# Attention in forty equal slots per row: jobs placed by a table, scores first in a slot

## The chip, the cores and the metric

The kernel runs on one core of a Trainium2 chip. The metric is the device time of one execution in microseconds. The engines are TensorE (PE in the views; PEld is its weight load), VectorE (DVE), ScalarE (ACT), GpSimd (POOL) and SyncE (SP, which only starts transfers). Each engine works through its own instructions in order and waits on semaphores for the others.

## The reference

```python
x = x + 0.5 * ffn(layernorm(x))       # x: 8 rows of 1024 tokens, 256 features
x = x + attn(layernorm(x))
x = x + 0.5 * ffn(layernorm(x))

# ffn: 8 experts of width 128, exact GELU, the two best experts of each token weighted by softmax
# attn, for each row of 1024 tokens, 8 heads of 64:
#   light: q, k, v = split(layernorm(x) * g + b) @ wqkv); windows of 64 queries see the window
#          before, their own and the next; softmax; @ wo_l
#   heavy: scores x @ rt_q and x @ rt_kv; the 256 best tokens by each (argsort);
#          rms-normed rows give hq, hk, hv; full 256 x 256 attention; @ wo_h,
#          added at the places of the chosen queries
```

## The kernel before, in words

Three stages follow each other: a feed-forward stage over 16 groups of 512 tokens (`ffn_group`), the attention over 8 rows (ROWS) of 1024 tokens, and the second feed-forward stage. Each engine's program is written out by hand, and the order in which they meet is the order of these programs.

A group of the feed-forward stage has ten steps s. In s = 0 to 7 PE multiplies one expert's first layer, ACT forms the GELU twice (`hf`, `hh`), POOL their difference (`hl`, L1302), and two steps later PE multiplies the second layer and DVE adds it to `xb` (L1056). In between stand the next group's statistics, norm, transposes, routing and gate. SP stores `xb` at a group's end and loads another.

The attention works on items: one item is a pair of heads (`hp`) of one tile of 128 queries. A row has 32 items of 8 light tiles (`t < T`) and 8 of 2 heavy tiles, 40 in all. An item goes through

- `scores` (PE, L631 light and L633 heavy): two matmuls, one for each head, into three banks (NS = 3) in turn;
- `maxima` (DVE, L1168/L1170), `exps` (ACT, L883), `reciprocals` (DVE, L1186), `prob_norm` (POOL, L1335: `prob` times `rden`);
- `turn` (PE, L642: four transposes of `prob`) three slots after the scores, `turned` (the copy into `probT`, ACT for even items, DVE for odd ones);
- `values` (PE, L656) four slots after; after the fourth pair of heads `oT_s` (ACT, L899), and the out projection `op` (PE, L667) six slots after, which DVE (L1200, light) or ACT (heavy) takes away.

Beside the items there are jobs, which share banks 6 and 7 in turn (`claim` waits until the job before the last has been taken away): `zt` (transposes of `z_row` into `xt`), `qkv` 0 to 24 (projections of q, k, V, six matmuls each: L464 to L466), `srow` (router scores along a row), `ga` and `hp` (the chosen rows and their projections) and `op`. Other engines have work for a row without PE: statistics of `x1` and `y_row` (DVE, `attn_stats1/2`), `rstd` and `row_norm` (POOL), `attn_y`, `attn_z`, `attn_yr` (ACT), `dot` (DVE, L1111: the router scores of a tile), `rank_piece` (DVE, L1134 to L1140: each token's place by counting larger scores; 16 pairs of pieces per row), `places`, then `scatter` (POOL, L1322: sixteen indirect transfers of `yr` to `hs_d`), SP's load of `hrow` (L421) and `tokens`. `heavy_add` (POOL, L1331) adds the heavy output to x2 in DRAM.

A row has 44 slots (`slots`, `items_of`, `attn_jobs`): LEAD = 4 slots without an item, in which 16 projections, `srow`, `ga` and `hp` are done; then 8 slots with the heavy items of the row before and the nine projections of V, all ranks of the row and the first scatter; then 32 slots (number s) with the light items, in which the next row is prepared. For row 0 statistics and norms stand between feed-forward groups 12 to 15, and the dots and `zt` behind group 15. SP's loop over the rows stores a finished row of x2 (L436), loads the next but one (`attn_load`, L459), and loads `hrow`; after the last light item it first loads back the feed-forward weights and the first three groups.

## Time and profile before

| | |
|---|---|
| Median of 3 runs | 2230.57 us (2229.94 to 2231.97) |
| Profiled execution, its own time | 2230.17 us |
| Its span in the trace | 2228.4 us |
| Mean granted clock of TensorE | 0.976 |
| PE busy | 2059.0 us, 92% |
| DVE busy | 1522.2 us, 68% |
| ACT busy | 1264.2 us, 57% |
| POOL busy | 1045.1 us, 47% |

Times in the trace count from the first instruction. The first feed-forward stage ends near 481.5 us and the second begins at 1785.3; the attention lies between. A busy share is an average over stages, so the rows below look at stretches.

Columns of the views: a window row has its bounds and length in us, then busy us (and instructions) of PE, PEld, DVE, ACT and POOL, PE's granted clock, the DMA engines' busy share and GB/s. A timeline row has start and duration in us, engine, line, operation, output<-inputs, form and count, and in brackets the idle time before it and what ended it; neighbours alike are merged. A wait row has the waiting engine and line, what it waited for, us in total, times and the longest.
### The profile page before, as it was taken

What the parts mean: (1) busy time and instruction counts of PE and PEld (TensorE: products, weight loads), DVE (VectorE), ACT (ScalarE), POOL (GpSimd) and SP (SyncE); (2) the same over time, 40 slices, a digit from 0 to 9 for tenths busy, and PEclk for the clock granted to TensorE, in tenths of its full rate; (3) what the DMA queues carried; (4) which work ended last, traced back from release to release, by engine and by line L of the source; (5) the groups of instructions that cost most, each with busy time, mean ns of one, the idle gap of its engine ahead of it and who ended that gap; (6) DMA issues with size and microseconds to landing.
All of it is one profiled execution on the core that took longest, in us unless ns stands there. A gap on an engine that the chain in (4) does not pass through costs nothing.

```text
span 2228.4 us, 40162 instructions
## 1 busy us (share of the span) xinstructions
PE 2059.0 (92%) x13232; PEld 1594.5 (72%) x13232; DVE 1522.2 (68%) x5207; ACT 1264.2 (57%) x2948; POOL 1045.1 (47%) x1150
## 2 busy tenths in 40 slices
PE   6999999869899899898998998998999699999998
PEld 5888888856576576675665665765766478888887
DVE  6888888667647657466376375476474368888887
ACT  4555555545846746646756656557556355555554
POOL 3444444443717617527427347257164244444444
PEclk9999999889999999999999999999999799999999
DMA  6111111001002011011011021020010311111110
GB/s 224 57 58 39 46 41 40 18 20 39 11 1 86 6 48 45 1 53 39 1 58 34 1 67 25 1 74 18 1 67 6 125 24 39 39 39 39 39 39 29
DMA packets 72326, 91.17 MB, mean 41 GB/s; under 512 B 6433, under 2 KB 66233, under 8 KB 71097
## 3 DMA queue, kind: packets, MB, share of 16 engines
q1 hardware_dynamic: 61368, 69.39, 9.3%
q0 software_dynamic: 8448, 18.95, 3.0%
q8 instruction: 107, 1.75, 0.3%
q14 instruction: 99, 0.80, 0.1%
q10 hardware_dynamic: 2304, 0.28, 0.1%
HBM read 40.23 MB, written 48.37 MB: 40 GB/s over the span
## 4 chain that ended last, share of the span: by engine, by line
PE 47%; POOL 18%; DVE 17%; issue 13%; ACT 5%; DMA 0%; POOLq 0%; DVEq 0%; ACTq 0%
PE bank L464 9%; PE bank L466 9%; PE bank L465 9%; POOL prob L1335 7%; POOL hs_d L1322 4%; PE bank L667 3%; PE bank L491 3%; PE bank L601 2%; PE bank L642 2%; PE bank L631 2%; PE bank L656 2%; ACT prob L883 2%; DVE xb L1056 2%; DVE st L968 2%; POOL hl L1302 2%
## 5 line engine op out<-in xcount | busy, mean ns | idle before, releaser
L1056 DVE SCALAR_TENSOR_TENSOR xb<-bank,gate,xb 128x256 f32<-128x256 f32 x1024 | 423.9, 477 | 122.8 <-PE bank L466 122.0
L1335 POOL TENSOR_TENSOR prob<-prob,rden 128x512 f32<-128x512 f32 x320 | 348.3, 1090 | 282.1 <-DVE rden L1186 278.5
L1302 POOL TENSOR_TENSOR hl<-hf,hh 128x512 fp32r<-128x512 f32 x256 | 330.5, 1299 | 232.8 <-ACT hh L758 223.9
L1168 DVE CUSTOM_DVE_ANT_0 prob<-bank,mask 128x256 f32<-128x256 f32 x512 | 197.0, 421 | 263.3 <-PE bank L631 259.3
L757 ACT ACTIVATE hf<-bank,b1s 128x512 f32<-128x512 f32 x256 | 176.5, 689 | 338.1 <-PE bank L466 330.7
L883 ACT ACTIVATE prob<-prob,nmax 128x256 f32<-128x256 f32 x512 | 255.8, 501 | 135.2 <-DVE nmax L1168 134.2
L464 PE MATMUL bank<-w_hi,hh 128*128 128x256 f32 x1024 | 295.9, 289 | 22.6 <-POOL hl L1302 20.4
L1322 POOL DMA_INDIRECT hs_d<-yr,place x128 | 130.5, 1019 | 361.0 <-DVE place L1149 339.9
L465 PE MATMUL bank<-w_hi,hl 128*128 128x256 f32 x1024 | 290.3, 284 | 0.0
L466 PE MATMUL bank<-w_lo,hh 128*128 128x256 f32 x1024 | 290.2, 283 | 0.0
L642 PE MATMUL bank<-ident,prob 128*128 128x128 f32 x1280 | 209.3, 288 | 50.2 <-POOL prob L1335 48.0
L464 PEld LDWEIGHTS bank<-w_hi,hh 128*128 128x128 f32 x1024 | 195.3, 191 | 45.5 <-POOL hl L1302 36.7
L464 PE MATMUL bank<-xt_hi,w_hi 128*128 128x512 f32 x512 | 215.6, 421 | 8.6 <-DVE w_lo L1088 8.3
L642 PEld LDWEIGHTS bank<-ident,prob 128*128 128x128 f32 x1280 | 149.0, 144 | 104.1 <-POOL prob L1335 80.7
L465 PE MATMUL bank<-xt_hi,w_lo 128*128 128x512 f32 x512 | 203.4, 397 | 0.0
L466 PE MATMUL bank<-xt_lo,w_hi 128*128 128x512 f32 x512 | 203.2, 397 | 0.0
L465 PEld LDWEIGHTS bank<-w_hi,hl 128*128 128x128 f32 x1024 | 196.1, 191 | 6.1
L466 PEld LDWEIGHTS bank<-w_lo,hh 128*128 128x128 f32 x1024 | 196.2, 192 | 0.0
L631 PE MATMUL bank<-kT,qT 64*128 64x256 f32 x1024 | 191.0, 443 | 0.8 <-ACT V L845 0.7
L656 PEld LDWEIGHTS bank<-probT,V 128*64 128x64 f32 x2048 | 111.6, 139 | 111.6 <-issue 100.2
L656 PE MATMUL bank<-probT,V 128*64 128x128 f32 x2048 | 173.4, 291 | 19.2 <-ACT oT_s L899 16.9
L758 ACT ACTIVATE hh<-bank,b1s 128x512 fp32r<-128x512 f32 x256 | 174.4, 681 | 0.0
(165 smaller groups left out, 4333.3 us busy)
## 6 DMA issues: line engine op xcount, KB each, us to landing
xb<-in_L_attn_x SPq DMA_DIRECT2D x16, 512.0 KB, 4.0
x_d<-xb SPq DMA_DIRECT2D x16, 512.0 KB, 2.9
x<-x_d SPq DMA_DIRECT2D x8, 1024.0 KB, 5.6
x_d<-x SPq DMA_DIRECT2D x8, 1024.0 KB, 4.4
xb<-x_d SPq DMA_DIRECT2D x16, 512.0 KB, 3.9
out<-xb SPq DMA_DIRECT2D x16, 512.0 KB, 2.9
hrow<-hs_d SPq DMA_DIRECT2D x16, 257.0 KB, 2.7
w_d<-w_hi SPq DMA_DIRECT2D x2, 1024.0 KB
```

Of the source, the lines that this page charges most:

```text
L464: pe.matmul(o, w[0], x[0], start=start, stop=False)
L465: pe.matmul(o, w[1], x[0], start=False, stop=False)
L466: return pe.matmul(o, w[0], x[1], start=False, stop=stop)
L631: ins = pe.matmul(bank[g % NS][:, 0:KEYS], qT[hs, hp, t * P:(t + 1) * P], kT[hs, hp, t * P:t * P + KEYS], start=True, stop=True)
L642: ins = pe.transpose(bank[3 + j % 2][:, (2 * h + kk) * P:(2 * h + kk + 1) * P], prob[j % NP][:, h, kk * P:(kk + 1) * P], ident[:, :])
L656: ins = pe.matmul(bank[5][h * DH:(h + 1) * DH, hp * P:(hp + 1) * P], V[:, t + kk, hs] if t < T else hv[:, kk, hs], probT[j % 2][:, 2 * h + ...
L883: act.activation(prob[j % NP][:, h, :], src, ACT.Exp, bias=nmax[:, j % 4, h:h + 1], scale=-1.0 if light else 1.0, accum_out=den[:, j % 4, ...
L1056: dve.scalar_tensor_tensor(out=x, in0=bank[ob][:, (t % 2) * D:(t % 2 + 1) * D], scalar=gate[:, k % 2, t, e:e + 1], in1=x, op0=ALU.mult, op ...
L1168: ins = dve.tensor_tensor_reduce(prob[j % NP][:, h, :], bank[g % NS][:, 0:KEYS], mask[:, which, :], -1.0, 3e38, ALU.add, ALU.min, nmax[:, ...
L1302: pool.tensor_tensor(hl[i % NH][:, :], hf[i % NH][:, :], hh[i % NH][:, :].bitcast(F32), ALU.subtract).then_inc(s_hl)
L1322: pool.indirect_dma_start(hs_d[r], bass.IndirectOffsetOnAxis(place[:, b, r, t:t + 1], 0), yr[:, t, :], None).then_inc(s_sct[r], 16)
L1335: pool.tensor_tensor(prob[j % NP][:, :, :], prob[j % NP][:, :, :], rden[:, j % 4, :].unsqueeze(2).broadcast_to([P, 2, KEYS]), ALU.mult).th ...
```

## The change

The 44 slots of a row become 40, every one with an item. Slots are numbered through (u), and each job has a function that names the slot in which it stands, relative to its row's first slot; the jobs of one row may lie in slots of the row before. `QKV_AT` puts the first 13 projections into slots -20 to -2 and the rest into 0 to 15. `qkv_at` orders them so that the first half of tokens of k, q and V comes first; they are written into the same `kT`, `qT` and `V` in two halves, and scores and values wait for the projection that they need (`qkv_with`) instead of for all. In a slot PE now does scores, first job, turn, second job, values, other jobs (before: first job, turn, second job, scores, third job, values, others); ACT takes exps first. Ranks go at 32 pieces over 26 slots, in row 0 at two pieces per slot in slots 0 to 10. Row 0's statistics, norms and half of its dots move into the feed-forward groups 12 to 15. The same jobs are done; before the second feed-forward stage its first statistics, norm, transposes, logits and gate stand later (`TAIL` is slot 32 of the last row).

```diff
-LEAD, B_SLOTS = 4, 32
-A_SLOTS = LEAD + 8
-HADD = 11
-SLOTS = A_SLOTS + B_SLOTS
+LIGHT, SLOTS = 32, 40
...
+        QKV_AT = (on(-20, 2, 1, 2), on(-14, 2, 1, 2), on(-8, 2, 1, 2, 1), on(0, 1, 2, 1), on(6, 1, 1, 2), on(11, 1, 2, 1))
...
+        def rank_slot(b, i):
+
+            if b == 0:
+                return i - 10 if i < 10 else (i - 10) // 2
+            return SLOTS * b - 19 + i * 26 // 32
...
             def project(b, i):
-                if i == 0:
-                    pe.wait_ge(s_xll, 4 * b + 4)
-                    if b == 0:
-                        pe.wait_ge(s_wlo, 7)
+
+                if i in (0, 12, 13):
+                    pe.wait_ge(s_xll, 4 * b + {0: 2, 12: 3, 13: 4}[i])
+                if i == 0 and b == 0:
+                    pe.wait_ge(s_wlo, 7)
...
                 if t < T:
-                    if t == 0 and hp == 0:
-                        pe.wait_ge(*left(("qkv", b, 24)))
-                        pe.wait_ge(*left(("qkv", b, 23)))
-                        if b == 0:
-                            pe.wait_ge(s_halo, 2)
+                    if hp == 0 and t in (0, 3, 4):
+                        pe.wait_ge(s_qkv, 25 * b + {0: qkv_with(0, 0), 3: qkv_with(1, 1), 4: qkv_with(0, 1)}[t])
+                    if j == 0:
+                        pe.wait_ge(s_halo, 2)
...
-            for i in range(4):
-                z_turn(0, i)
-            for b, a in slots():
-                todo = attn_jobs(b, a)
+            for u in slots():
+                todo = attn_jobs(u)
+                if is_item(u):
+                    scores(u)
                 for what in todo[0:1]:
                     job(*what)
-                if item_back(b, a, 3) is not None:
-                    turn(item_back(b, a, 3))
+                if is_item(u - 3):
+                    turn(u - 3)
                 for what in todo[1:2]:
                     job(*what)
-                if items_of(b, a) is not None:
-                    scores(b, a)
-                for what in todo[2:3]:
-                    job(*what)
-                if item_back(b, a, 4) is not None:
-                    values(item_back(b, a, 4))
-                for what in todo[3:]:
+                if is_item(u - 4):
+                    values(u - 4)
+                for what in todo[2:]:
                     job(*what)
...
+                    if k in (12, 13) and 2 <= s < 6:
+                        attn_stats1(k - 12, s - 2)
+                    if k in (14, 15) and 2 <= s < 6:
+                        attn_stats2(k - 14, s - 2)
+                    if k == 15 and 2 <= s < 10:
+                        dot(0, (s - 2) // 2, s % 2)
...
+                    if k in (12, 13) and s == 7:
+                        rstd(1, k - 12, k - 12)
+                    if k in (14, 15) and s == 7:
+                        rstd(2, k - 14, 2 * (k - 14))
+                        row_norm(k - 14)
...
-                if b == ROWS and a == LEAD + 1:
+                if u == TAIL + 7:
                     ffn_stats(GROUPS)
```

Three places show how instructions move. The first is VectorE where row 0's first items begin (`prob`, `nmax`: maxima; `junk`, `sjunk`: rank pieces; `probT`: the copy of a turn). Before:

```order
L1138 SCALAR_TENSOR_TENSOR sjunk,rank_76<-srow,scol,later 128x128
L1140 SCALAR_TENSOR_TENSOR sjunk,rank_76<-srow,scol,not_later 128x128
L1144 TENSOR_REDUCE rank<-rank_76 128x8
L1168 ISA prob_108,nmax<-bank,mask 128x256
L1168 ISA nmax 128x1
L1168 ISA prob_108,nmax<-bank,mask 128x256
L1168 ISA nmax 128x1
L1149 CAST place<-rank 128x8
L1168 ISA prob_109,nmax<-bank,mask 128x256
L1168 ISA nmax 128x1
L1168 ISA prob_109,nmax<-bank,mask 128x256
L1168 ISA nmax 128x1
```

and now:

```order
L1203 ISA prob_108,nmax<-bank,mask 128x256
L1203 ISA nmax 128x1
L1169 TENSOR_SCALAR junk,rank_76<-srow,scol 128x640
L1171 TENSOR_SCALAR junk,rank_76<-srow,scol 128x256
L1173 SCALAR_TENSOR_TENSOR sjunk,rank_76<-srow,scol,later 128x128
L1175 SCALAR_TENSOR_TENSOR sjunk,rank_76<-srow,scol,not_later 128x128
L1203 ISA prob_109,nmax<-bank,mask 128x256
L1203 ISA nmax 128x1
L1203 ISA prob_109,nmax<-bank,mask 128x256
L1203 ISA nmax 128x1
L1221 RECIPROCAL rden<-den 128x2
L1169 TENSOR_SCALAR junk,rank_76<-srow,scol 128x768
```

The ranks of row 0 stood in front of the first item; now two pieces stand between the maxima of one item and the next.

The second is GpSimd at the heavy add of row 0 (`x_d<-ho,token`) and the preparation of row 2 (`tri`, `rn`: `rstd` and `row_norm`; `prob`: the multiply of an item; `hs_d`: a scatter). Before:

```order
L1335 TENSOR_TENSOR prob_110<-prob_110,rden 128x512
L1331 DMA x_d<-ho,token 1024x256
L1335 TENSOR_TENSOR prob_111<-prob_111,rden 128x512
L1335 TENSOR_TENSOR prob_108<-prob_108,rden 128x512
L1335 TENSOR_TENSOR prob_109<-prob_109,rden 128x512
L1331 DMA x_d<-ho,token 1024x256
L1335 TENSOR_TENSOR prob_110<-prob_110,rden 128x512
L1268 TENSOR_SCALAR tri_71<-mv_73 128x4
L1269 TENSOR_SCALAR tri_71<-mv_73 128x4
L1271 TENSOR_TENSOR tri_71<-tri_71,cols 128x4
L1274 TENSOR_TENSOR tri_71<-tri_71 128x4
L1283 TENSOR_TENSOR rn<-mv_73 128x4
```

and now:

```order
L1367 TENSOR_TENSOR prob_111<-prob_111,rden 128x512
L1363 DMA x_d<-ho,token 1024x256
L1354 DMA hs_d<-yr,place 1024x257
L1294 TENSOR_SCALAR tri_71<-mv_73 128x4
L1295 TENSOR_SCALAR tri_71<-mv_73 128x4
L1297 TENSOR_TENSOR tri_71<-tri_71,cols 128x4
L1300 TENSOR_TENSOR tri_71<-tri_71 128x4
L1309 TENSOR_TENSOR rn<-mv_73 128x4
L1311 TENSOR_TENSOR rn<-rn,mv_73 128x4
L1313 TENSOR_SCALAR rn<-rn 128x4
L1315 TENSOR_TENSOR rn<-rn,cols 128x4
L1317 TENSOR_SCALAR rn<-rn 128x4
```

A heavy add, a scatter, `rstd` and `row_norm` now follow on one another between two multiplies of `prob`; before, several multiplies lay between them, and no scatter.

The third is TensorE at heavy items beside projections (`hk,hq`: scores; `ident,prob`: turn; `probT`: values). Before:

```order
L642 MATMUL bank<-ident,prob_111 128x128 x4
L633 MATMUL bank<-hk,hq 128x256 x2
L656 MATMUL bank<-probT_112,hv 64x128 x4
L464 MATMUL bank<-wqkv_hi,xt_hi 128x512
L465 MATMUL bank<-wqkv_hi,xt_lo 128x512
L466 MATMUL bank<-wqkv_lo,xt_hi 128x512
L464 MATMUL bank<-wqkv_hi,xt_hi 128x512
L465 MATMUL bank<-wqkv_hi,xt_lo 128x512
L466 MATMUL bank<-wqkv_lo,xt_hi 128x512
L642 MATMUL bank<-ident,prob_108 128x128 x4
L464 MATMUL bank<-wqkv_hi,xt_hi 128x512
```

and now:

```order
L669 MATMUL bank<-hk,hq 128x256 x2
L501 MATMUL bank<-wqkv_hi,xt_hi 128x512
L502 MATMUL bank<-wqkv_hi,xt_lo 128x512
L503 MATMUL bank<-wqkv_lo,xt_hi 128x512
L501 MATMUL bank<-wqkv_hi,xt_hi 128x512
L502 MATMUL bank<-wqkv_hi,xt_lo 128x512
L503 MATMUL bank<-wqkv_lo,xt_hi 128x512
L678 MATMUL bank<-ident,prob_109 128x128 x4
L696 MATMUL bank<-probT_112,V 64x128 x4
L669 MATMUL bank<-hk,hq 128x256 x2
L707 MATMUL bank<-wol,oT_s 128x256 x4
```

The scores stood behind the projection and the turn of their slot; now they stand ahead of both, and turn and values follow each other.

## Rows read from the trace of the kernel before

**Rows 1.** Windows: a steady row, and the end of the attention.

```profile
985.40:1143.42 158.02, 147.13 (x952) 101.98 (x950) 95.74 (x404) 98.01 (x272) 78.45 (x88) 0.99 0.11 33
1737.90:1785.30 47.40, 28.88 (x176) 19.50 (x177) 17.61 (x64) 15.79 (x47) 11.39 (x14) 0.75 0.40 146
```

**Rows 2.** Timeline of SP: stores of groups 11, 12 and 13 to 15.

```profile
357.91 0.36 SPq L392 DMA_DIRECT2D x_d<-xb  x1
...
385.08 0.36 SPq L392 DMA_DIRECT2D x_d<-xb  x1
...
418.59 65.36 SPq L392 DMA_DIRECT2D x_d<-xb  x3
```

**Rows 3.** Timeline of PE at the head of group 13.

```profile
391.00 0.58 PE L464 MATMUL bank<-w_hi,hh 128*128 128x256 f32 x1 [4.68 <-POOL hl L1302]
```

**Rows 4.** Timeline of PE at the start of the attention.

```profile
491.60 1.09 PE L551 MATMUL bank<-ident,z_row 128*128 128x128 f32 x4 [8.96 <-ACT xf_t L828]
...
498.46 0.80 PE L464 MATMUL bank<-xt_hi,wqkv_hi 128*128 128x512 f32 x1 [3.96 <-POOL xt_lo L1312]
```

**Rows 5.** Waits of PE in the steady row of rows 1.

```profile
PE bank L642 <- POOL prob L1335: 6.6, 9, 2.7
```

**Rows 6.** Timeline of PE: a light item, a heavy item with a projection.

```profile
998.76 1.28 PE L633 MATMUL bank<-hk,hq 64*128 64x256 f32 x4
999.97 0.66 PE L656 MATMUL bank<-probT,hv 128*64 128x128 f32 x8
1000.56 0.50 PE L464 MATMUL bank<-wqkv_hi,xt_hi 128*128 128x512 f32 x1
...
1002.06 0.60 PE L642 MATMUL bank<-ident,prob 128*128 128x128 f32 x4
...
1017.82 1.99 PE L667 MATMUL bank<-woh,oT_s 128*128 128x256 f32 x8
1019.65 0.60 PE L642 MATMUL bank<-ident,prob 128*128 128x128 f32 x4
1020.18 0.70 PE L631 MATMUL bank<-kT,qT 64*128 64x256 f32 x4
1020.82 0.66 PE L656 MATMUL bank<-probT,V 128*64 128x128 f32 x8
```

**Rows 7.** Timelines of DVE and PE at the end of the attention.

```profile
1752.25 1.41 DVE L968 BATCH_NORM_STATS2 st<-xb 128x6 f32<-128x256 f32 x4 [9.73 <-DMA xb<-x_d]
...
1755.12 1.22 PE L633 MATMUL bank<-hk,hq 64*128 64x256 f32 x2 [9.46 <-ACT prob L883]
```

**Rows 8.** Timeline of DVE: ranks before row 0's items, ranks among items.

```profile
511.10 0.34 DVE L1134 TENSOR_SCALAR_CACHE_REDUCE junk<-srow,scol 128x128 uint8<-128x128 f32 x1
...
512.57 0.35 DVE L1140 SCALAR_TENSOR_TENSOR sjunk<-srow,scol,not_later 128x128 uint8<-128x128 f32 x1
...
512.85 0.47 DVE L1134 TENSOR_SCALAR_CACHE_REDUCE junk<-srow,scol 128x256 uint8<-128x256 f32 x1
...
669.68 1.12 DVE L1140 SCALAR_TENSOR_TENSOR sjunk<-srow,scol,not_later 128x128 uint8<-128x128 f32 x1
```

**Rows 9.** Timeline of POOL at the same place among items.

```profile
669.60 1.05 POOL L1335 TENSOR_TENSOR prob<-prob,rden 128x512 f32<-128x512 f32 x1 [1.25 <-DVE rden L1186]
670.81 1.01 POOL L1322 DMA_INDIRECT hs_d<-yr,place  x1 [0.16 <-issue]
```

**Rows 10.** POOL: groups by form from 550 to 1780, then timeline.

```profile
L1331 POOL DMA_INDIRECT x_d<-ho,token x14 | 22.8, 1629 | 3.0 <-issue 3.0
...
1048.96 0.30 POOL L1268 TENSOR_SCALAR tri<-mv 128x4 f32<-128x4 f32 x1
...
1053.61 2.04 POOL L1335 TENSOR_TENSOR prob<-prob,rden 128x512 f32<-128x512 f32 x2
```

**Rows 11.** Timeline of SP: store of a finished row, load of another.

```profile
825.86 0.36 SPq L436 DMA_DIRECT2D x_d<-x  x1
830.26 0.36 SPq L459 DMA_DIRECT2D x<-x_d  x1
```

More of the change, by code:

```diff
@@ new lines, in is_item, with due, on @@
+        def is_item(u):
+            return 0 <= u < SLOTS * ROWS
+        TAIL = SLOTS * ROWS - 8
+        def due(u, slot_of, count):
+            return [(b, i) for b in range(ROWS) for i in range(count) if slot_of(b, i) == u]
+        def on(first, *steps):
+            return tuple(itertools.accumulate(steps, initial=first))
+        QKV_AT = (on(-20, 2, 1, 2), on(-14, 2, 1, 2), on(-8, 2, 1, 2, 1), on(0, 1, 2, 1), on(6, 1, 1, 2), on(11, 1, 2, 1))
+        QKV_AT = tuple(itertools.chain(*QKV_AT))
@@ L305, in build @@
                     job_no[job] = len(job_no)
-        for job in row_jobs0():
-            job_no[job] = len(job_no)
-        for b_, a_ in slots():
-            for job in attn_jobs(b_, a_):
+        for u_ in slots():
+            for job in attn_jobs(u_):
                 job_no[job] = len(job_no)
@@ L1370, in pool_program @@
                 ffn_group(k, GROUPS - 1)
-                if k in (12, 13):
-                    rstd(1, k - 12, k - 12)
-                if k in (14, 15):
-                    rstd(2, k - 14, 2 * (k - 14))
-                    row_norm(k - 14)
-            for i in range(4):
-                xl_lo(0, i)
             pool.wait_ge(s_wlo, 6)
```

297 lines of the change are left out of this document (144 added, 153 removed).

## Prediction

> **What bounds the kernel now.** I read the windows by stage first. TensorE (PE) is the engine to follow: in a steady row of the attention it is busy 147.13 of 158.02 us, while VectorE (DVE) and ScalarE (ACT) have some 96 and 98 us of work and GpSimd (POOL) 78 [rows 1]. The change adds and removes no matmul, so it can only win or lose time in which PE stands. That time lies in four places.
>
> First, the last groups of the first feed-forward stage. Stores of groups follow each other in 27.16 us (357.91 to 385.08); the next comes 33.5 us later, and the third (the end of the merged row, 418.59 + 65.36, less its own 0.36) 98.5 us after the first, where three regular groups take 81.5: 17.0 us too much [rows 2]. The timeline shows how: PE stood 4.68 us for POOL's `hl` at the head of a group [rows 3], because DVE's statistics and POOL's `rstd` of the coming row were put between two groups.
>
> Second, the start of the attention. After the last expert matmul PE transposes four of the eight `z_row` blocks, waits 8.96 us, and the first projection begins only at 498.46, after another 3.96 us [rows 4].
>
> Third, the rows. 10.9 us of a steady row are PE's idle time, and 6.6 of them are the transposes of `prob` waiting for POOL [rows 5]. Part of the waiting hides in PE's busy rows: a heavy item's two score matmuls take 1.21 us from their start to the next operation's (998.76 to 999.97) where a light item's take 0.64 (1020.18 to 1020.82), since the second head waits for ACT's exp of the item before [rows 6]. I put that at 1.6 us per row, and a row's avoidable waits at 10.9 + 1.6 = 12.5 us.
>
> Fourth, the end. From the last values of item 311 (1737.90, when SP may load the weights) to the second feed-forward stage at 1785.30 there are 47.4 us, with PE busy for 28.88 at a granted clock of 0.75 [rows 1]. DVE waits 9.73 us for the load of `xb`, which lands at 1752.25, 14.35 us after its queue was released; DVE works in order, so the maxima behind it are late and PE stands 9.46 us [rows 7].
>
> **The change, part by part.** Prices of PE, from start to start [rows 6]: out projection 1.83, turn 0.53, scores 0.64, values 0.59, one projection (six matmuls) 1.50. A slot without a job is 1.8 us, one with a projection 3.3, with projection and out projection 5.1. Splitting the projections up costs nothing: 1.50 is already the price of one alone between other kinds.
>
> *Feed-forward groups 12 to 15.* The statistics, `rstd` and norms now stand inside the groups at s = 2 to 9, where POOL has two slots (s = 8, 9) without `hl`. DVE is given 8 dots in the last group, which has no next group's statistics, route and gate to do. I leave 3 of the 17.0 us: **-14**.
>
> *Start.* Statistics, norms and half of the dots are done within the feed-forward groups, so ACT can fill `xt` right after the last group; still, POOL's `xl_lo` now stands behind the wait for the last store and the memsets of `kT`, and the first projection behind the score rows, whose last eight dots follow the feed-forward stage. I count 6 us of standing for the 8.96 + 3.96 of before and the waits and slow matmuls between them: **-7**.
>
> *Row 0.* Its ranks are now spread at two pieces per slot over slots 0 to 10. Two pieces (one `srow` compare pair and one diagonal pair) take 1.75 us when POOL is quiet (511.10 to 512.85) [rows 8]. But the diagonal pair reads two SBUF tensors, and its second half took 1.12 us where POOL's `prob` multiply (669.60) had started 0.08 us before it, against 0.35 alone: 0.77 more [rows 8, 9]. In the new order each pair follows the reciprocal that releases this multiply. DVE's items cost 1.1 us a slot: a steady row's 95.7 us [rows 1] less 28 for 16 such double pieces and some 24 for dots, statistics and collisions, over 40 slots. In slots 0 to 10 it has 11 by 1.1 plus 11 by 1.75 plus 6.5 for the statistics of row 1, 37.9 us, or 46.3 with 0.77 on each pair; PE has 29.2 (11 scores, 8 turns, 7 values, 8 projections and an out projection, by the prices above). So DVE sets the pace: 8 to 17 us, of which two are absorbed by the three score banks. I take 12, and 3 more for the rest of the row, against some 11 us of waits in row 0 before: **+4**.
>
> On that collision the Trainium skill ("SBUF — State Buffer", "SBUF: two separate sides") says that a DVE operation with two SBUF inputs and a GpSimd operation that reads SBUF exclude each other for a whole instruction. By that rule every pair collides and the end of the range for row 0 is the 17; the trace agrees where they overlap.
>
> *Rows 1 to 6.* The scores stand first in a slot, before the job and the turn. The maxima, exps and the `prob` multiply then come at least 0.53 us earlier against the turn three slots on; slots are 3.6 us on the mean (146 us of PE's work over 40), where a light item of before, a quarter of an out projection included, has 2.2. So most POOL waits go, and the hidden one of heavy scores. What is late next: POOL in slots 8 to 11 has two heavy adds (1.63 each), scatters (1.0 each), twice `rstd` and `row_norm` (1048.96 to 1053.61: 4.65) and its four multiplies of 1.05 [rows 9, 10]: 3.3 + 4.1 + 9.3 + 4.2 = 20.9 us where PE has 13.5; the multiply for a turn may lag some 4 us before PE stands, so 2 to 3 us per row are lost there, with ACT's norms waiting for the second `rstd`. DVE has in slots 2 to 6 two statistics per slot beside 1.2 rank pieces: 14.5 to 17 us against 15.3 of PE: about 1. Slots 19 and 20 hold ga, score rows, zt and hp, and their two shared banks are emptied by ACT: about 1. With 1.5 for the rest a row waits 6, not 12.5: 6 rows by 6.5, **-39**.
>
> *Row 7* has no next row behind it; its 5 to 7 us of waits shrink to 3: **-3**.
>
> *End.* `ffn_stats` moves from two slots behind the values of item 311 to four behind, after the maxima of item 319. Its load comes at the same 14.35 us, so heavy items 316 to 319 run before it, 4 by 2.4 us. Then the chain statistics 1.8, `rstd` 1.8, norm 1.1, turn, copies and subtraction about 3, logits 1.9, and the last out projection 1.8 go to 28.5 us after the release instead of 47.4. Less work of PE remains behind the release too (about 4 us), which is no gain: **-15**.
>
> Sum: -14 -7 +4 -39 -3 -15 = -74 us. Against the profiled execution's 2230.17 us (span 2228.4) and the median of 2230.57, which are equal here: **2156 us**.
>
> **The rivals.** (A) The forecast, 2135 to 2180: 0.62.
>
> (B) The waits of the rows stay. A slot of POOL with heavy add, scatter, `rstd` and `row_norm` is 1.05 + 1.63 + 1.02 + 4.65 = 8.4 us, more than two slots of PE, and dots and diagonal pairs meet POOL's multiplies more often than before (in the trace of before the ranks lie mostly in front of the items). Against it: a turn has two slots of room. If rows 1 to 6 keep their 12.5 us, the sum loses 39: 2195; range 2180 to 2218: 0.18.
>
> (C) The waits of the rows nearly vanish (2 per row) and row 0 loses only its 8: 6 by 4 and 8 better: 2124; 2110 to 2135: 0.12. For it speaks that no engine but PE has more than 111 us of work in a row of 146.
>
> (D) Slower. DVE takes things in order: in a slot with an out projection (eight light tiles per row, 64 in all) it stands at the tile's add until PE has done this slot's last job, then does reciprocal, rank pieces, dots or statistics, and only then the next maxima; PE's second score matmul of the next slot needs the first of these, with three score banks. If each of the 64 cost PE 1.2 us, all 74 would be gone; 1.3 us, and it is slower (2240). The tail behind the add is 0.4 + 0.1 + 1.75 + 0.7 = 3 us at most slots against 3.3 of the next slot, so I expect some 0.2: 0.05. In the same direction: the load of the next row's `x1`, which follows a store of 4.4 us of the same size [rows 11], is now needed five slots after the last light tile and not nine; DVE's first statistics would stand for it, and the maxima behind them. It lands about 2 us early; it would have to be 13 late in six rows. 0.01.
>
> (E) The gains are eaten exactly: 0.02.
>
> **How the numbers follow.** Likeliest: A, 2156. 2118 to 2198 holds A, most of C and about half of B, near 0.8; A's own range is 2135 to 2180. Faster by over 0.2% (4.5 us, what a measurement of this kernel can tell): A, B and C, 0.92. Same 0.02, slower 0.06.
>
> **What would show it.** Stores of the feed-forward groups 27 to 28 us apart through group 15. The first item about 30 us nearer to the start. DVE without a pause and PE waiting for `nmax` in row 0's first eleven slots. Row period (SP's store of `x`) near 152 us. PE's remaining waits for `prob` gathered in slots 8 to 13, none of heavy scores. 28 to 30 us from SP's weight loads to the second stage. The prediction is wrong if the rows keep a period of 158, or if PE waits in all slots for `nmax`.

## The result, and the profile after

The changed kernel takes 2158.86 us (median of 4 runs, 2156.79 to 2159.13) against 2230.26 us for the kernel before (2229.53 to 2231.97, run beside it): ratio 0.9678, interval 0.9666 to 0.969. The span went from 2228.4 to 2157.3 us, 71.1 less. The forecast was 2156.

SyncE's timeline of the changed kernel gives the stages:

```profile
385.07 0.36 SPq L429 DMA_DIRECT2D x_d<-xb  x1
412.22 52.11 SPq L429 DMA_DIRECT2D x_d<-xb  x3
...
636.88 0.36 SPq L473 DMA_DIRECT2D x_d<-x  x1
...
792.86 0.36 SPq L473 DMA_DIRECT2D x_d<-x  x1
...
943.81 0.36 SPq L473 DMA_DIRECT2D x_d<-x  x1
...
1099.81 0.36 SPq L473 DMA_DIRECT2D x_d<-x  x1
...
1251.01 0.36 SPq L473 DMA_DIRECT2D x_d<-x  x1
...
1561.44 0.36 SPq L473 DMA_DIRECT2D x_d<-x  x1
...
1679.43 0.34 SPq L466 DMA_DIRECT2D w_hi<-w_d  x1
```

The last of the three merged stores of feed-forward groups starts at 412.22 + 52.11 - 0.36 = 463.97. Against the same events before:

| stretch (us) | before | after | forecast, change | measured, change |
|---|---|---|---|---|
| store of group 12 to store of group 15 | 98.5 | 78.9 | -14 | -19.6 |
| to the store of row 0's x (start and row 0) | 185.9 | 172.9 | -7 +4 | -13.0 |
| rows 1 to 6 | 951.6 | 924.6 | -39 | -27.1 |
| row 7, to the weight loads | 116.8 | 118.0 | -3 | +1.2 |
| weight loads to the second feed-forward stage | 47.4 | 33.8 | -15 | -13.6 |
| second feed-forward stage | 443.1 | 444.1 | 0 | +1.0 |

Windows of the changed kernel, to be read against [rows 1]:

```profile
496.00:636.88 140.88, 133.89 (x844) 93.26 (x842) 105.33 (x427) 90.33 (x256) 72.34 (x84) 0.98 0.07 22
...
792.86:943.81 150.95, 142.49 (x952) 100.07 (x950) 102.19 (x404) 95.39 (x271) 76.76 (x88) 1.00 0.11 34
943.81:1099.81 156.00, 146.06 (x952) 102.44 (x950) 104.30 (x404) 95.35 (x271) 77.05 (x88) 0.98 0.11 33
...
1679.43:1713.19 33.76, 25.66 (x157) 19.40 (x157) 12.09 (x39) 11.72 (x32) 8.01 (x11) 0.76 0.57 206
```

The rows are of two kinds, near 151 and near 156 us (one lies between, at 154.4), and VectorE, whose work did not change, is busy 102 to 104 us in a row where it was busy 95.7. Rows 1 to 6 as one window, before and after:

```profile
669.46:1621.09 951.63, 888.91 (x5702) 616.05 (x5700) 576.37 (x2414) 588.39 (x1627) 469.73 (x528) 0.98 0.11 33
636.88:1561.44 924.56, 868.45 (x5702) 609.76 (x5700) 620.98 (x2414) 572.00 (x1626) 461.78 (x528) 0.99 0.11 34
```

Of the 27.1 us, 20.5 are busy time of TensorE and only 6.6 idle time (62.7 to 56.1, or 10.5 to 9.4 a row). Half of the busy time is that of the heavy score matmuls, before and after:

```profile
L633 PE MATMUL bank<-hk,hq 64*128 64x256 f32 x192 | 44.6, 428 | 0.0
L669 PE MATMUL bank<-hk,hq 64*128 64x256 f32 x192 | 33.8, 428 | 0.0
```

One matmul takes 428 ns in both, but the second head follows the first sooner: this is the hidden wait of the forecast, 10.8 us where it had 6 by 1.6. TensorE's waits over the whole run, first the largest of the kernel before, then those of the changed kernel:

```profile
PE bank L642 <- POOL prob L1335: 48.0, 73, 3.0
```

```profile
PE bank L707 <- ACT V L883: 15.2, 6, 2.5
...
PE bank L615 <- DVE scol L1146: 12.5, 8, 3.9
PE bank L696 <- ACT oT_s L937: 10.5, 15, 1.4
...
PE bank L667 <- ACT prob L921: 9.5, 7, 1.4
...
PE bank L667 <- DVE nmax L1203: 4.2, 4, 2.0
PE bank L678 <- POOL prob L1367: 4.1, 7, 0.7
```

The waits of the turn for POOL's `prob`, 6.6 us of a steady row [rows 5] and 48.0 of the whole run before, are 4.1 in the whole run. Other waits have taken most of their place. New is the first line: six times 2.5 us, once a row, the out projection of slot 13 stands for its bank, which ACT has not emptied of a projection of V. New, too, are the score rows that stand for VectorE's last dots (`scol`) and the light scores that stand for the exp of a heavy item (L667 for ACT's `prob`, 1.35 us at each row's start). VectorE's maxima are late in 4.2 us only.

**The two kinds of rows.** The same wait is in both. The out projection behind it, in a row of 156 us and in one of 151:

```profile
1000.30 3.57 PE L707 MATMUL bank<-wol,oT_s 128*128 128x256 f32 x8 [2.54 <-ACT V L883]
...
1155.01 1.97 PE L707 MATMUL bank<-wol,oT_s 128*128 128x256 f32 x8 [2.53 <-ACT V L883]
```

and windows there, in the first row and in the second:

```profile
953.00:957.00 4.00, 4.00 (x21) 2.58 (x20) 2.35 (x9) 1.04 (x3) 1.55 (x2) 0.61 0.27 99
...
1002.00:1005.00 3.00, 3.00 (x19) 2.19 (x17) 1.09 (x3) 2.50 (x7) 2.67 (x3) 0.68 0.46 74
...
1109.00:1113.00 4.00, 4.00 (x29) 2.94 (x28) 3.31 (x14) 1.85 (x7) 2.27 (x3) 1.00 0.19 69
...
1158.00:1161.00 3.00, 3.00 (x19) 2.15 (x18) 1.47 (x7) 2.70 (x10) 2.82 (x3) 1.00 0.54 88
```

(two stretches of each row, behind its start and behind slot 13). In the row of 156 us the granted clock is partly or wholly at the lower level (1.2 GHz) in two stretches: behind the wait at the row's start (1.35 us for the exp of a heavy item) and behind the one of slot 13. With the same waits the next row keeps 2.4 GHz. Of the six rows two have no such stretch (150.95 and 151.20 us), three have two of about 4 us each (155.98 to 156.00), and row 6 has one of 7 us, behind slot 13 (154.43). Of the 5.05 us between the two rows shown, 3.6 are TensorE's busy time (146.06 for 142.49) and 1.5 are waits.

**The held dots.** The timeline of VectorE in that first row:

```profile
1008.35 2.90 DVE L1146 CUSTOM_DVE_ANT_0 scj<-y_row,rts 128x256 f32<-128x256 f32 x1
```

and that of GpSimd at the same time:

```profile
1007.67 0.99 POOL L1354 DMA_INDIRECT hs_d<-yr,place  x1 [0.17 <-issue]
1008.68 1.29 POOL L1344 TENSOR_TENSOR xt_lo<-xf_t,xt_hi 128x512 fp32r<-128x512 f32 x1
1009.92 1.05 POOL L1367 TENSOR_TENSOR prob<-prob,rden 128x512 f32<-128x512 f32 x1
```

A dot that takes 0.41 us alone took 2.90, up to the end of a subtraction and a multiply of GpSimd that follow each other without a gap. The scatter in front of them is not what held it. The next dot lay wholly beside another scatter:

```profile
1011.41 0.43 DVE L1146 CUSTOM_DVE_ANT_0 scj<-y_row,rts 128x256 f32<-128x256 f32 x1
```

```profile
1011.13 1.00 POOL L1354 DMA_INDIRECT hs_d<-yr,place  x1 [0.17 <-issue]
```

In rows 1 to 6, 22 dots met a scatter and nothing else of GpSimd, and each took 0.42 or 0.43 us; nine of the 96 took 2.16 to 2.96 us, and all nine met the subtraction and the multiply behind it. The score rows, which need the last dot, stand 1.1 us in this row and 1.7 us in the quiet one; VectorE waits for TensorE twice between this dot and the last, so this wait isn't the 2.90 us carried on.

### The profile page after: what moved, and what is told of

Same layout as the page of the kernel before. It is cut to its first block, busy times and chain, and to the rows that moved or that the text cites. A ratio compares the mean times of both kernels' runs of the same rounds, so it can differ in the third digit from the quotient of the medians.

```text
span 2157.3 us, 40188 instructions
## 1 busy us (share of the span) xinstructions
PE 2032.7 (94%) x13232; PEld 1586.8 (74%) x13232; DVE 1581.0 (73%) x5207; ACT 1243.2 (58%) x2948; POOL 1036.4 (48%) x1150
## 4 chain that ended last, share of the span: by engine, by line
PE 57%; DVE 20%; issue 10%; POOL 8%; ACT 4%; DMA 0%; DVEq 0%; POOLq 0%; ACTq 0%
PE bank L501 10%; PE bank L503 9%; PE bank L502 9%; PE bank L707 5%; PE bank L696 5%; PE bank L667 4%; PE bank L678 4%; PE bank L639 3%; PE bank L528 3%; DVE st L996 3%; DVE xb L1084 2%; POOL tri L1297 2%; POOL hl L1328 2%; DVE wt L1056 2%; DVE scj L1146 2%
## 5 line engine op out<-in xcount | busy, mean ns | idle before, releaser
L1367 POOL TENSOR_TENSOR prob<-prob,rden 128x512 f32<-128x512 f32 x320 | 335.9, 1051 | 548.4 <-DVE rden L1221 546.2
L667 PE MATMUL bank<-kT,qT 64*128 64x256 f32 x1024 | 191.7, 431 | 13.7 <-ACT prob L921 9.5
L1215 DVE COPY probT<-bank 128x512 f32<-128x512 f32 x160 | 110.2, 689 | 128.5 <-PE bank L678 128.3
L678 PE MATMUL bank<-ident,prob 128*128 128x128 f32 x1280 | 197.9, 278 | 4.2 <-POOL prob L1367 4.1
L678 PEld LDWEIGHTS bank<-ident,prob 128*128 128x128 f32 x1280 | 157.3, 143 | 59.2 <-issue 18.8
```

What stands on the lines that cost most here:

```text
L667: ins = pe.matmul(bank[g % NS][:, 0:KEYS], qT[hs, hp, t * P:(t + 1) * P], kT[hs, hp, t * P:t * P + KEYS], start=True, stop=True)
L678: ins = pe.transpose(bank[3 + j % 2][:, (2 * h + kk) * P:(2 * h + kk + 1) * P], prob[j % NP][:, h, kk * P:(kk + 1) * P], ident[:, :])
L1367: pool.tensor_tensor(prob[j % NP][:, :, :], prob[j % NP][:, :, :], rden[:, j % 4, :].unsqueeze(2).broadcast_to([P, 2, KEYS]), ALU.mult).th ...
```

## The experiments

Times of the changed kernel from here on are 2158.9 us, ratio 0.968. Each run was compared with the kernel before beside it; the ratio is of that pair.

### e1: scores late

```diff
-                if is_item(u):
-                    scores(u)
                 for what in todo[0:1]:
                     job(*what)
                 if is_item(u - 3):
                     turn(u - 3)
                 for what in todo[1:2]:
                     job(*what)
+                if is_item(u):
+                    scores(u)
```

> The changed kernel with one part undone: within a slot the order of the kernel before (first job, turn, second job, scores, values on TensorE; ScalarE's exps behind the evacuations). The forty slots, the placement of projections, ranks and norms stay. Theory S (what the forecast for the rows rests on: scores first gives the multiply of GpSimd its lead over the turn three slots on): TensorE's waits for prob come back, some 5 us in each of seven rows, and the second head of heavy scores waits for an exp again, 1 to 2 us per row; the period of a row goes from 154 to 158-160 us: 2185 to 2200 us. Rival T (the lead comes from the projections that now stand between the items, so slots last 3.6 us on the mean and the order inside one is indifferent): 2158 to 2166 us, waits for prob under 12 us in the whole run, period 154 to 155.

Measured 2179.79 us, ratio 0.9772 (0.9757 to 0.9787): +21, between the two and nearer to S. Rows 1 to 6 take 942.2 us (157.0 each, 17.6 more in all), row 0 with the start 5.5 us more, and the waits for `prob` are back:

```profile
PE bank L615 <- DVE scol L1150: 25.5, 8, 3.9
PE bank L678 <- POOL prob L1371: 23.2, 29, 2.2
```

So the order in the slot carries most of the gain of the rows (17.6 of 27.1 us). The waits for `prob` are 19.1 us longer, and those of the score rows, which neither theory named, 13.0; others are shorter (15.2 to 7.4 us for V, and the 9.5 us for the exp at the row's start are gone). How much each is worth is not separated.

### e8: scores first, alone, in the kernel before

```diff
+                if items_of(b, a) is not None:
+                    scores(b, a)
                 for what in todo[0:1]:
                     job(*what)
                 if item_back(b, a, 3) is not None:
                     turn(item_back(b, a, 3))
-                for what in todo[1:2]:
-                    job(*what)
-                if items_of(b, a) is not None:
-                    scores(b, a)
-                for what in todo[2:3]:
+                for what in todo[1:3]:
                     job(*what)
```

> The kernel before with one part of the change alone: in a slot TensorE does the scores first and ScalarE the exps first. All else (forty-four slots with projections in front of the items, ranks, norms) is the kernel before. In the changed kernel undoing this order cost 21 us. Theory U (the order is worth the same here): the waits for prob, 6.6 us per row of before, and the hidden ones of heavy scores go, 8 rows by 3 to 5: -20 to -40 us: 2190 to 2210 us. Rival W (without projections between the items a slot of 1.8 to 2.2 us is too short for GpSimd's multiply whatever the order): 0 to -12 us, waits for prob stay above 30 us in the run.

Measured 2210.29 us, ratio 0.9907 (0.9892 to 0.9922): -20. Rows 1 to 6 give 13.4 of it. U holds at its weak edge, and the waits tell why it was not more:

```profile
PE bank L656 <- ACT oT_s L897: 37.4, 54, 1.3
PE bank L633 <- ACT prob L881: 21.4, 9, 11.5
...
PE bank L642 <- POOL prob L1331: 9.3, 14, 1.9
```

The turn's waits fell from 48.0 to 9.3 us, but the values now stand 37.4 us for `oT_s` where they stood 20.4, and heavy scores 21.4 us for an exp where they stood 10.3: the item behind is reached sooner. Even so the order is worth nearly the same in both kernels, 20 us here and 21 in e1 (in rows 1 to 6 13.4 and 17.6). So the spread of the projections over forty slots adds little to it; the rest of the gain of the rows, 10 to 14 of 27.1 us, comes with the rest of the change and not with the order.

### e2: preparation of row 0 back between the groups

```diff
                 ffn_group(k, GROUPS - 1)
+                if k in (12, 13):
+                    for q in range(TG):
+                        attn_stats1(k - 12, q)
```

(and likewise the second statistics, norms, `rstd`, `row_norm` and eight dots).

> The changed kernel with the first row's statistics, rstd, norms and the first eight dots put back between the feed-forward groups 12 to 15 and behind group 15. Theory P (the term of the feed-forward groups is a stall of its own): the time from the store of group 12 to that of the last group goes from 78.9 back to 98 us, and the start is 2 to 5 us longer because the dots follow the last group: 2179 to 2184 us. Rival Q (part of the gain there comes from something else in the changed kernel, and the start takes the work back): 2165 to 2172 us. Rival R (the start's 13 us also come from these statistics): 2190 to 2195 us.

Measured 2189.62 us, ratio 0.9821 (0.9806 to 0.9836): +31, just under rival R's range. SyncE's timeline:

```profile
385.98 0.36 SPq L429 DMA_DIRECT2D x_d<-xb  x1
420.03 65.86 SPq L429 DMA_DIRECT2D x_d<-xb  x3
...
665.63 0.36 SPq L473 DMA_DIRECT2D x_d<-x  x1
```

From the store of group 12 to the last: 420.03 + 65.86 - 0.36 - 385.98 = 99.55 us, 20.6 more; start and row 0: 180.1 us, 7.2 more. The term of the feed-forward groups is separate and all there, and 7.2 of the 13.0 us of start and row 0 come from this preparation too, about half of what R says. The 5.5 us that e1 gives back in the same stretch are nearly all of the rest.

### e3: row 0's ranks in front of its items

```diff
             if b == 0:
-                return i - 10 if i < 10 else (i - 10) // 2
+                return i // 2 - 16
```

> The changed kernel with row 0's 32 rank pieces in the slots -16 to -1, two per slot, and none beside items. Theory F (the forecast's step: pairs beside items collide with GpSimd's multiply and cost row 0 some 12 us): TensorE loses its 4 us of nmax waits and the busy rows shorten, but 16 pairs of 1.75 us are 28 us in front of item 0 where TensorE has 13 projections of 1.5 and the zt jobs, so it stands 6 to 8 us there: sum -6 to 0, 2153 to 2159 us. Theory G (row 0's pairs cost only the 4.2 us that the chain of waits shows): the loss of 6 to 8 us in front of item 0 stands against 4: +2 to +6 us, 2161 to 2165 us, with the first scores unchanged near 494 us and the first waits for nmax at items 1 and 2.

Measured 2165.47 us, ratio 0.971 (0.9697 to 0.9723): +6.6, just above G. The row of TensorE's timeline that explains it:

```profile
508.42 1.22 PE L667 MATMUL bank<-kT,qT 64*128 64x256 f32 x2 [9.62 <-DVE nmax L1203]
```

Ranks beside items are much the cheaper place: 4.2 us of waits in exchange for these 9.6.

### e4: GpSimd's lump pulled apart

```diff
         def hadd_slot(b, kk):
-            return SLOTS * (b + 1) + 8 + 3 * kk
+            return SLOTS * (b + 1) + (6 + 9 * kk if b + 1 < ROWS else 8 + 3 * kk)
...
+        def norm_slot(b, g):
+            return SLOTS * b + (-32, -28)[g]
```

> The changed kernel with GpSimd's lump in slots 8 to 11 of a row pulled apart: heavy adds of the row before at slots 6 and 15 instead of 8 and 11 (the last row's stay), and row_norm one slot behind the first and three behind the second rstd of the second normalization. Theory K (in the rows of 156 us ScalarE stands 2.8 us for the second rstd, evacuates V late, the out projection of slot 13 waits 2.5 us for its bank, and TensorE's clock is at its lower level behind it): the wait goes, all six rows have 151 us: -10 to -18 us, 2141 to 2149 us, granted clock 1.00 in every row. Rival L (the rows of 156 come from another thing, such as DVE's late score rows at slot 20 or the shift of the prob buffers): the wait at slot 13 goes but the period stays 154: 2155 to 2159 us.

Measured 2152.81 us, ratio 0.9649 (0.9636 to 0.9662): -6. Both were partly wrong: the wait of slot 13 became shorter (1.58 us in five rows, 2.26 in one, for 2.53) but stayed, and rows 2 to 6 became equal, near 153.5 us. Each of them has two stretches of lower granted clock; these now follow the wait at the row's start (1.35 us) and one of the score rows for the dots (1.83 us at slot 20), and none follows slot 13. TensorE's timeline at slot 13 in the row of the longest wait:

```profile
996.90 1.97 PE L710 MATMUL bank<-wol,oT_s 128*128 128x256 f32 x8 [2.26 <-ACT V L886]
```

and ScalarE's just before:

```profile
994.21 1.09 ACT L838 ACTIVATE z_row<-y_row,tri 128x256 f32<-128x256 f32 x2 [2.88 <-POOL tri L1303]
```

ScalarE meets the second `rstd` one slot after VectorE's aggregates of the same half; however free GpSimd is, that is too soon. ScalarE then comes late to the exps and to V, behind it in its order, and the out projection stands for the bank.

### e5: ScalarE's second norms two slots later

```diff
         def z_slot(b, q):
-            return SLOTS * b - 31 + q // 2
+            return SLOTS * b - 31 + q // 2 + (2 if q >= TG else 0)
```

> The changed kernel with one edit: ScalarE's four norms of the second half of z_row stand two slots later (13 and 14 of a row instead of 11 and 12); rstd, row_norm and heavy adds stay where they are. The run before moved GpSimd's work and the wait of 2.3 to 2.5 us at the out projection of slot 13 stayed, since ScalarE stood 2.9 us at the norm of slot 11 for the second rstd all the same. Theory M (that wait comes from where ScalarE meets the second rstd): the waits of the out projection for V (15.2 us in six rows) go, and with them the stretches of lower granted clock in the rows of 156 us; rows of 148.5 to 150 us, together -20 to -30 us: 2129 to 2139 us. Rival N (only the wait itself is worth something, the clock's dips have other causes): -8 to -14 us: 2145 to 2151 us. Rival O (another wait takes its place, such as the turn's for prob behind the lump of GpSimd): 0 to -5 us.

Measured 2145.93 us, ratio 0.9627 (0.9614 to 0.964): -13, rival N's figure. The 15.2 us for V are gone; in their place:

```profile
PE bank L678 <- POOL prob L1367: 17.9, 22, 1.8
```

Two rows of it, in windows:

```profile
791.00:941.88 150.88, 142.89 (x952) 99.94 (x950) 102.62 (x404) 95.48 (x271) 76.77 (x88) 1.00 0.11 34
941.88:1094.29 152.41, 144.44 (x952) 100.92 (x950) 102.53 (x404) 95.58 (x271) 76.79 (x88) 0.99 0.11 34
```

A quiet row is not faster than before this edit (150.9 against 151.0): there the new waits for `prob` are as long as those taken away. What is gained is the slow stretch of slot 13: three rows have one stretch left, behind the row's start, and 152.4 to 152.9 us instead of 156, and row 6 has none (150.9 instead of 154.4). M was wrong on the size, N on its reason.

### e6: the reciprocal last in VectorE's slot

```diff
-                if is_item(u - 1):
-                    reciprocals(u - 1)
...
                         for r in range(2):
                             dot(b, t, r)
+                if is_item(u - 1):
+                    reciprocals(u - 1)
```

> The changed kernel with VectorE's reciprocal (which releases GpSimd's multiply of prob) behind this slot's rank pieces, statistics and dots instead of in front of them. Theory D (the dots and diagonal pairs of VectorE are held while GpSimd's multiply reads SBUF, which makes VectorE's 96 us of a row 104 and the score rows at slot 20 wait 1 to 4 us for scol): VectorE's busy time falls to 98 us per row or less, the waits of the score rows for scol shrink by 4 us or more in the run, and the multiply, up to 1.75 us later, is still in time for the turn: -4 to -10 us. Rival H (the multiply is then late for the turn in the slots with ranks and dots): VectorE's busy time falls too, but waits of the turn for prob come back, 2 to 4 us per row: +8 to +20 us.

Measured 2137.81 us, ratio 0.9586 (0.9573 to 0.9599): -21, more than twice what D gave. VectorE is busy 93.46 us in a row, by the window of one:

```profile
940.57:1090.86 150.29, 144.02 (x952) 100.93 (x950) 93.46 (x403) 95.67 (x271) 76.58 (x88) 0.99 0.12 35
```

VectorE's groups by form over rows 1 to 6 (the dots, and the second half of the diagonal pairs) of the changed kernel:

```profile
L1146 DVE CUSTOM_DVE_ANT_0 scj<-y_row,rts 128x256 f32<-128x256 f32 x96 | 77.0, 802 | 6.9
...
L1175 DVE SCALAR_TENSOR_TENSOR sjunk<-srow,scol,not_later 128x128 uint8<-128x128 f32 x96 | 80.7, 840 | 0.0
```

and of this run:

```profile
L1146 DVE CUSTOM_DVE_ANT_0 scj<-y_row,rts 128x256 f32<-128x256 f32 x96 | 57.0, 594 | 6.9
...
L1175 DVE SCALAR_TENSOR_TENSOR sjunk<-srow,scol,not_later 128x128 uint8<-128x128 f32 x96 | 33.9, 353 | 0.0
```

The pairs' second half went from 840 to 353 ns (46.8 us in all; their first half rose from 335 to 408, which takes 7.1 us back), the dots from 802 to 594. The waits for `prob` came back to 17.5 us, as H said, and cost less than was won. In row 0, where the pairs are thickest, the waits for `nmax` went from 4.2 to 1.7 us, and start and row 0 together stayed as long (173.7 us against 172.9).

### e9: the dots alone in front of the reciprocal

The same edit for the dots only.

> The changed kernel with only the dots of VectorE (16 per row, slots 11 to 18) in front of the slot's reciprocal; rank pieces and statistics stay behind it. All three in front gave -21 us, with VectorE's busy time of a row down from 104 to 94 us. Theory X (what costs TensorE time is the dots' lag, by the late maxima and score rows behind them): VectorE's busy time falls by some 5 us per row, and -12 to -18 us, 2141 to 2147 us. Rival Y (the diagonal pairs, 16 per row in slots 21 to 46, carry most of it): -2 to -7 us, 2152 to 2157 us.

Measured 2142.49 us (2138.83 to 2151.29), ratio 0.9608 (0.9588 to 0.9629): -16, theory X in time. Not in its detail: VectorE's rows fell by 2.5 us, not 5, since only the dots became shorter. Their group in rows 1 to 6:

```profile
L1146 DVE CUSTOM_DVE_ANT_0 scj<-y_row,rts 128x256 f32<-128x256 f32 x96 | 62.3, 649 | 6.9
```

and the window of a row:

```profile
944.08:1094.08 150.00, 142.56 (x952) 100.16 (x950) 100.64 (x404) 95.49 (x271) 76.73 (x88) 1.00 0.11 35
```

With 15 us less of held dots rows 1 to 6 took 18 us less. About 8 of these are shorter waits in rows of the same kind (150.0 for 150.95, 153.15 for 156), and 10 come because four rows have no slow stretch, 150.0 to 150.3 us, where the changed kernel had two; the other two have two stretches each, 153.15. A stretch costs 1.5 us in this run. The waits that precede them (1.35 and 2.77 us) are in all six rows. The number of stretches probably differs from execution to execution: the five of this run go from 2138.83 us at a mean granted clock of 0.989 to 2151.29 at 0.985, and the profiled one is near the fast end.

What the 40 us of the pairs are worth isn't isolated. With the pairs and the statistics in front as well (e6) the profiled spans are the same, 2137.8 and 2137.9, but the medians are 4.7 us apart (2137.81 and 2142.49). The waits for `prob` are 13.4 us longer in e6 and others shorter (for the exp at the row's start 9.5 to 4.1 us, for V 16.7 to 14.2, for `nmax` 4.2 to 1.7). So putting them in front is worth about 5 us as the edit stands; what the late multiply costs would come on top, at most 13.4 us.

### e7: the end, closer to the values

```diff
-                if u == TAIL + 7:
+                if u == TAIL + 5:
                     ffn_stats(GROUPS)
```

(with memset, `rstd`, norms, transposes, logits and gate one to two slots earlier).

> The changed kernel with the work of the second feed-forward stage's first group at its old distance from the values of item 311: VectorE's statistics two slots behind them instead of four (before the maxima of items 318 and 319), memset, rstd, norms, transposes, logits and gate one to two slots earlier as well. Theory E (the forecast: the statistics wait for a load that lands some 14 us after its release and hold back the maxima behind them): the first maxima behind them are late, TensorE stands 3 to 8 us more for nmax, and the end goes from 33.8 us to 38-42: +4 to +8 us. Rival I (the load is in by then, since the slots are shorter and fewer now, and the chain simply starts earlier): -1 to -4 us.

Measured 2162.66 us, ratio 0.9692 (0.9679 to 0.9705): +4, at E's edge. VectorE's timeline behind the release:

```profile
1697.09 1.41 DVE L996 BATCH_NORM_STATS2 st<-xb 128x6 f32<-128x256 f32 x4 [9.10 <-DMA xb<-x_d]
```

and TensorE's:

```profile
1699.95 1.22 PE L669 MATMUL bank<-hk,hq 64*128 64x256 f32 x2 [9.03 <-ACT prob L921]
```

The stall of [rows 7] is back nearly in full, yet the end takes 36.3 us, only 2.5 more than the changed kernel's 33.8 (and row 7 1.5 more). In the changed kernel other waits stand in its place (3.5 us for `probT`, 3.1 for the norm), both behind the same load. Its 33.8 is a long one: in the runs that leave this part alone the end takes 30.0 to 32.0 us, so the earlier statistics cost 4 to 6 us against those.

### e10, e11, e12: together

> The changed kernel with both edits that helped: ScalarE's second half of z_row two slots later (-13 us alone) and VectorE's reciprocal last in a slot (-21 us alone). Theory A2 (two separate losses, the out projection's wait for ScalarE and VectorE's collisions): -28 to -34 us, 2125 to 2131 us. Rival B2 (moving ScalarE's norms brought waits of the turn for prob of 17.9 us, and the late reciprocal as many; both load the same place, GpSimd in slots 8 to 12, so the gains don't add): -20 to -25 us, 2134 to 2139 us.

Both edits in one kernel: measured 2133.98 us, ratio 0.9565 (0.9552 to 0.9579): -25, B2. Waits for `prob`: 24.1 us.

> The two edits of the run before together with GpSimd's heavy adds at slots 6 and 15 and its row_norm one and three slots behind the two rstd (-6 us alone). Theory A3 (the turn's waits for prob in slots 8 to 13 come from GpSimd's lump): they fall under 8 us in the run, and it is 5 to 8 us faster than the run before: 2118 to 2126 us if that one is at 2128. Rival B3 (what is left is the late release of the multiply, not the lump): within 2 us of the run before.

With the edits of GpSimd's lump as well: measured 2122.39 us, ratio 0.9512 (0.9499 to 0.9525): the fastest of all, 36 us under the changed kernel and 12 under e10. A3 in its direction, with more than its 5 to 8 us; its figure for the waits was wrong (16.5 us, not under 8). The window of a row:

```profile
931.41:1079.71 148.30, 142.67 (x952) 100.26 (x950) 94.98 (x403) 95.55 (x271) 77.13 (x88) 1.00 0.12 35
```

The last one differs from the first of these three in VectorE's order:

```diff
                 for b, i in due(u, rank_slot, 32):
                     rank_piece(b, i)
+                for b, t in due(u, dot_slot, T):
+                    if b > 0 or t >= TG:
+                        for r in range(2):
+                            dot(b, t, r)
+                if is_item(u - 1):
+                    reciprocals(u - 1)
```

> The kernel of run e10 with one difference: the reciprocal stands behind rank pieces and dots but in front of the statistics, which read one SBUF tensor and weren't seen to be held by the multiply (1.4 us for four). Theory A4 (in the slots of the statistics, 2 to 5 and 7 to 10, the multiply then starts 0.7 us or more earlier, and the turn's waits of 1.9 to 2.3 us near slot 10 shrink): 3 to 6 us faster than e10. Rival B4 (those waits come from heavy add, rstd and row_norm): within 2 us of e10.

Measured 2126.57 us, ratio 0.9529 (0.9516 to 0.9542): 7 us under e10, A4 and a little more; waits for `prob` 20.3 us. Rows 1 to 6 give 5.2 of it; in e10 each has one stretch of lower clock, here only one has, and that row takes no longer than its neighbours (149.56 and 149.57 us). Whether this and the spread of GpSimd's work add was not tried.

## Why the prediction was right, and where it was off

**The sum and its sign.** -74 forecast, -71 measured. Three terms are off by 6 to 12 us: two gained 16 us more than forecast, the rows 12 less, and the last three stretches together 7 less. That the total is within 3 us is luck.

**Feed-forward groups: right in kind, -14 for -19.6.** The step "three regular groups take 81.5" was too high a floor: the last group prepares no other, and groups 13 to 15 take 78.9 us. Nothing of the 17.0 us stayed, where 3 were left. The runs show that this term is separate (20.6 us with the preparation put back).

**Start and row 0: -3 for -13.0.** The start stands nearly as forecast (3.3 us for `zt`, 3.9 for the dots; 6 were counted). The first scores came at 493.96 us for 538.56 before, 44.6 us nearer and not the 30 that the prediction gave as a sign, since twelve of the projections and most ranks now stand behind them. If the start gave its 7 us, row 0 gained 6 where it was to lose 4. By the runs 7.2 of the 13.0 us are the preparation's and 5.5 the order's in the slot. The failed step is "DVE sets the pace: 8 to 17 us ... I take 12". VectorE was without a pause (34.17 of 35.04 us busy from 493.96 to 529), as said, but eleven slots took 31.7 us against TensorE's 29.2, and row 0 from 496 us on has 7.0 us of idle TensorE, not 15. The early ranks (e3) give the sign, and the late reciprocal (e6) bounds what the collisions of the pairs, the 0.77 us each that led from 8 to 17, cost through VectorE's pace: 2.5 us of waits for `nmax`. That the three score banks take up the rest is argued, not shown.

**Rows 1 to 6: -39 for -27.1.** That the order brings the gain is shown from both sides (17.6 us lost without it, 13.4 gained by it alone). The hidden waits of heavy scores went as priced (10.8 us for 9.6), and the waits for `prob` went too, 40.4 to 4.1 us in these rows. The size failed in the step "a row waits 6, not 12.5": TensorE stands 9.4 us a row on the mean, against 10.5 before, or 12.3 with the hidden wait. A quiet row waits 8.5 us (150.95 less 142.49), but is busy for 142.5 and not the 146 that were used, so at 151 it beats the forecast's 152. Three rows have two slow stretches and end at 156, one has a long one and ends at 154.4.

The terms of that 6 compare as follows in a quiet row. For GpSimd's lump, with ACT's norms waiting for the second `rstd`, 2 to 3 us were forecast, and 3.3 came: 0.8 for `prob` and 2.5 as a wait for a bank, through V in ScalarE's order. The size was near, the place was not foreseen. For slots 19 and 20 and just behind them about 1 us was forecast, and 3.3 came: 1.7 of the score rows for the dots, 1.3 for `xf_t`, 0.3 for `srow`. The collision had been applied to the pairs of row 0 and not to the dots of each row, which lie in slots 11 to 18 beside GpSimd's lump and just ahead of the score rows; with the dots in front (e9) the wait of the score rows is 0.5 us. The exp at the row's start, 1.35 us, was not named, and the 1 us for VectorE in slots 2 to 6 did not come.

The clock was not priced at all. In the changed kernel the rows with two stretches of lower clock take 5 us more than the quiet ones. In e9 two stretches cost 3.1 us (153.15 against 150.0 to 150.3), in e12 one cost nothing. The 1.5 us of longer waits in a row of 156 us (1.9 for 0.5 us at `oT_s`, 1.4 for 0.7 at `xf_t`, less at the score rows) come where the stretch of slot 13 has shifted TensorE against GpSimd and VectorE; that the shift is their cause is argued, not shown.

On these collisions the Trainium skill ("SBUF — State Buffer", "SBUF: two separate sides") has an exclusive lock that the loser waits for a whole instruction. The row of 2.90 us shows more than one instruction: two GpSimd operations back to back before the dot went through. That such operations delay VectorE is borne out by this case (dots take 0.41 us alone and 0.80 on the mean of rows 1 to 6); that the delay sets the time is borne out for the dots, and for the pairs only to about 5 us.

**Row 7 and the second stage: -3 and 0 for +1.2 and +1.0.** Small, and not studied.

**End: -15 for -13.6.** Right as a sum, not in its detail. The forecast put this stretch at 28.5 us and took 4 us off the gain for work that moves ahead of the release; it took 33.8. The durations that it lists add up to 25.8 with the load's 14.35, not to 28.5. The step that gave the stall to the statistics' place is only partly so: putting it back costs 4 us in all, not the 9.5 of the wait. The rest of the 13.6 was not taken apart.

**Rivals.** B is nearer to what happened than its chance of 0.18 says. The rows' idle time hardly fell (10.5 to 9.4 us), and the two causes that B named cost time: GpSimd's lump, met by ScalarE at the second `rstd` (13 us by e5), and the dots that meet GpSimd's operations (16 us by e9). The rows gained all the same, by TensorE's busy time. D's late maxima were hardly seen (4.2 us), and E and C did not come.

## What to carry to other kernels

When one engine must release another (here the reciprocal the multiply), put work of its own that the released engine's operation would hold up ahead of the release, not behind it; but price such a collision only where somebody stands behind it: 15 us less of held dots went with 18 us less in the rows (10 of them where slow rows became quiet), 40 us less of held pairs with about 5 by the medians. A wait of an engine in order reaches the critical path through whatever is queued behind it, so for each moved wait list the evacuations that follow it. Where TensorE's rows differ by a few per cent at equal work and equal waits, compare the granted clock of quiet and slow rows before looking for another wait. And count a gain in idle and in busy time: here most of the rows' gain was in what the profile calls busy.

## What the hardware showed that was not expected

- A 0.41 us dot on VectorE was held 2.90 us, to the end of a 1.29 us subtraction and a 1.05 us multiply of GpSimd that followed each other without a gap. Beside a scatter alone 22 dots took 0.42 to 0.43 us.
- The granted clock fell behind a wait of 2.54 us in one row and not behind one of 2.53 us in the next, by the same program with the same work. What decides between them stays open; in the profiled executions the changed kernel has seven such stretches in rows 1 to 6, the one with dots first four, the fastest version one.
- A stretch of lower clock does not always lengthen a row: 1.5 us each in e9, nothing in e12, where the row's waits for `prob` are 0.8 us shorter than its neighbour's (2.5 and 3.3 us).
